# Four graph layers in one kernel: mask and row maximum fused on VectorE, first normalisation on ScalarE, output projection in float32, all orders rewritten, no loop

## The reference

```python
h = jnp.maximum(_layernorm(x, axis=-1), 0.0)
x = x + _L0_gnn_ref(h, L0_gnn_w_qkv, L0_gnn_w_proj, L0_gnn_b_proj, L0_gnn_ln_gamma, L0_gnn_ln_beta, adj)
h = jnp.maximum(_layernorm(x, axis=-1), 0.0)
x = x + _L1_gnn_ref(h, adj, L1_gnn_Wq, L1_gnn_Wk, L1_gnn_Wv)
h = jnp.maximum(_layernorm(x, axis=-1), 0.0)
x = x + _L2_gnn_ref(h, L2_gnn_W, L2_gnn_a, L2_gnn_beta, adj)
h = jnp.maximum(_layernorm(x, axis=-1), 0.0)
x = x + _L3_gnn_ref(h, adj, L3_gnn_weight, L3_gnn_bias)
```

```python
attn = jnp.einsum('bhnd,bhmd->bhnm', q, k) * scale
attn = jnp.where(attn_mask[None, None] == 0, -jnp.inf, attn)
attn = jax.nn.softmax(attn, axis=-1)
o = jnp.einsum('bhnm,bhmd->bhnd', attn, v).transpose(0, 2, 1, 3).reshape(b, n, d)
o = o @ w_proj + b_proj
```

## Time and profile before

| what | value |
|---|---|
| median of 3 runs | 1529.49 us (1529.12 to 1531.04) |
| the profiled execution, its own time | 1527.43 us |
| its span, first to last instruction | 1525.4 us |
| PE busy | 1482.7 us, 97% of the span, 16392 matmuls |
| DVE busy | 1301.0 us, 85% |
| ACT busy | 1120.1 us, 73% |
| POOL busy | 661.3 us, 43% |
| mean granted TensorE clock | 0.994 |

### The profile page before, as it was taken

The page is one execution under the profiler, slowest core; times in us unless marked ns, Lnnn a source line. Parts: engine busy times, 40 slices in busy tenths (PEclk is TensorE's granted clock), DMA queues, the critical chain, the costliest instruction groups (busy, mean ns, idle before and its releaser), DMA issues.

```text
span 1525.4 us, 46270 instructions
## 1 busy us (share of the span) xinstructions
PE 1482.7 (97%) x16392; PEld 1375.0 (90%) x16392; DVE 1301.0 (85%) x3726; ACT 1120.1 (73%) x2884; POOL 661.3 (43%) x981
## 2 busy tenths in 40 slices
PE   6989999999999999999989999999999999999996
PEld 5879999999999999999989999999999999999985
DVE  3888888888888888888888898898898898898895
ACT  4667777777777777777767777777777777777763
POOL 2244444444444444444444444444444444444442
PEclk9999999999999999999999999999999999999999
DMA  3000010000000010000010010010000010000001
GB/s 107 15 16 15 23 30 22 23 29 22 23 30 22 23 29 22 23 29 23 23 31 18 28 29 18 27 30 18 28 30 19 26 30 20 25 29 22 17 16 35
DMA packets 38102, 39.84 MB, mean 26 GB/s; under 512 B 2416, under 2 KB 37488, under 8 KB 37872
## 3 DMA queue, kind: packets, MB, share of 16 engines
q1 hardware_dynamic: 37872, 36.84, 7.9%
HBM read 20.05 MB, written 16.78 MB: 24 GB/s over the span
## 4 chain that ended last, share of the span: by engine, by line
PE 94%; DVE 2%; issue 2%; ACT 1%; POOL 1%; DMA 0%; POOLq 0%; DVEq 0%; ACTq 0%
PE bank L325 41%; PE mid L360 7%; PE mid L325 6%; PE mid L372 5%; PE bank L384 4%; PE mid L388 4%; PE mid L365 4%; PE mid L446 4%; PE mid L534 4%; PE mid L423 4%; PE bank L341 3%; PE bank L474 3%; PE mid L341 2%; PE mid L452 1%; PE bank L458 1%
## 5 line engine op out<-in xcount | busy, mean ns | idle before, releaser
L557 ACT ACTIVATE probs<-mid,neg_max 128x128 f32<-128x128 f32 x1024 | 295.3, 423 | 49.9 <-DVE neg_max L797 49.9
L897 POOL TENSOR_TENSOR rstd<-var_eps,minus_half 128x2 f32<-128x2 f32 x320 | 244.0, 763 | 25.1
L927 POOL TENSOR_TENSOR xb<-x,b_proj_beta 128x512 f32<-128x512 f32 x64 | 82.7, 1293 | 283.1 <-DVE o_res L807 283.1
L895 POOL TENSOR_TENSOR var_eps<-mean_var,eps 128x2 f32<-128x2 f32 x320 | 104.2, 326 | 167.1 <-DVE mean_var L717 167.1
L912 POOL TENSOR_TENSOR inv_norm<-sum_sq,minus_half 128x2 f32<-128x2 f32 x64 | 44.1, 689 | 260.8 <-DVE sum_sq L772 260.8
L730 DVE SCALAR_TENSOR_TENSOR h_t_lo<-bank,h_t_hi 128x512 fp32r<-128x512 f32 x128 | 88.4, 691 | 79.1 <-ACT h_t_hi L650 55.4
L713 DVE BATCH_NORM_STATS2 stats<-x 128x6 f32<-128x256 f32 x384 | 143.3, 414 | 5.8 <-DMA x<-in_x 3.6
L360 PE MATMUL mid<-ident,probs 128*128 128x128 f32 x1024 | 144.0, 275 | 3.7 <-ACT probs L557 3.7
L724 DVE TENSOR_SCALAR z<-x,mean_var,rstd 128x256 f32<-128x256 f32 x384 | 141.2, 410 | 2.7 <-POOL rstd L897 2.7
L360 PEld LDWEIGHTS mid<-ident,probs 128*128 128x128 f32 x1024 | 117.7, 142 | 4.8 <-ACT probs L557 4.8
L384 PE MATMUL bank<-probs_t,v 128*32 128x128 f32 x2048 | 105.9, 278 | 6.6 <-issue 6.0
(11 more groups left out here) (149 smaller groups left out, 5649.5 us busy)
## 6 DMA issues: line engine op xcount, KB each, us to landing
x<-in_x SPq DMA_DIRECT2D x64, 256.0 KB, 2.7
out_x<-x SPq DMA_DIRECT2D x64, 256.0 KB, 2.2
w_qkv_sb<-in_w_qkv SPq DMA_DIRECT2D x1, 768.0 KB, 4.5
w_q_sb<-in_w_q SPq DMA_DIRECT2D x1, 256.0 KB, 4.4
w_k_sb<-in_w_k SPq DMA_DIRECT2D x1, 256.0 KB, 4.7
w_v_sb<-in_w_v_t SPq DMA_DIRECT2D x1, 256.0 KB, 5.6
w_proj_sb<-in_w_proj SPq DMA_DIRECT2D x1, 256.0 KB, 5.8
w_gat_x<-in_w_gat SPq DMA_DIRECT2D x1, 256.0 KB, 6.1
```

The costliest lines, as they stand in the source:

```text
L557: last = act.activation(probs[:, r, s], mid[:, r, s * N:(s + 1) * N], ACT.Exp, bias=neg_max[:, r, s:s + 1])
L895: pool.tensor_tensor(var_eps[:, k], mean_var[:, k, :, 1], eps[:], ALU.add).then_inc(ln_eps[k], 1)
L897: pool.tensor_tensor(rstd[:, k], var_eps[:, k], minus_half[:], ALU.pow).then_inc(ln_rstd[k], 1)
L927: pool.tensor_tensor(xb[:], x0[:, i1], both(b_proj_beta), ALU.add).then_inc(xb_ready, 1)
```

## The change

Five things are changed.

1. **Mask and maximum.** The four mask matmuls are gone and each score matmul writes its own part of the bank (`start=True, stop=True`). `q_t` is scaled by -SCALE, so the banks hold the negated scores. VectorE runs, for each of the 16 heads of a pair, one `tensor_tensor_reduce` that adds +1e30 where there is no edge, stores the sum in `masked` in SBUF, and keeps the minimum of each row as `neg_max`. Ahead of every four of them stands a memset of one element. The program lists each as two instructions: the operation itself, and one that writes out `neg_max`. The two `tensor_reduce` are gone. ScalarE's exponentials read `masked` from SBUF, with scale -1.
2. **First z.** `z0` moves from VectorE to ScalarE, as z = x * rstd + shift with a small `shift0` from VectorE (one instruction of 128 x 2).
3. **Output projection in float32.** `o_t_hi`, `o_t_lo` and the split of `w_proj` are gone; the projection is 4 float32 matmuls of 256 columns in place of 12 in fp32r.
4. **Orders, banks and distances.** Each engine's step is written in a new order, and nearly all products use other banks. The four transposes of probabilities go to banks of their own in place of `mid`. Several parts move to an earlier step of a pair: `q` and `k` to `on[0]`, heads, `rel_v`, `z1` transposes, `hw`, `u` and `y_t` each one step earlier on TensorE. The distance from load to store stays eight steps.
5. **No loop, early constants.** All 71 steps are written out. The late constants are made ahead of step 2 on VectorE and POOL, and TensorE waits for them ahead of step 4 (all three: step 5 before). The fold of `w_q` and `w_k` runs ahead of step 0's transposes on TensorE (ahead of step 1 before).

```diff
-    STEPS = 28
-    FIRST = STREAMS + (PAIRS - STREAMS) % STEPS
...
-            for t in range(FIRST):
+            for t in range(PAIRS + STREAMS - 1):
                 for made_by, make in set_up:
                     if made_by == t:
                         make()
                 step(t, t % 2, streams(t))
-            with eng.Fori(FIRST, PAIRS - STEPS + 1, STEPS) as t:
-                for i in range(STEPS):
-                    step(t + i if i else t, i % 2, [True] * STREAMS)
...
             def scores():
-                for r in range(RG):
-                    pe.matmul(mid[:, r], ident_b[:], mask_b[:].unsqueeze(1).to_broadcast([128, BC, N]),
-                              start=True, stop=False)
...
-                                             k_t[at, hc, b * N:(b + 1) * N], start=False, stop=s == BC - 1,
+                                             k_t[at, hc, b * N:(b + 1) * N], start=True, stop=True,
...
+                if on[2]:
+                    pe.wait_ge(o_norm_ready, done(p2))
+                    bank_free(pe, (o_norm_ready, p2, 1), (probs_t_ready[0], p2, 1))
+                    rows_f32(halves(o_bank), lambda b, c: o_t[:, b, c], w_proj_sb).then_inc(o_psum, 1)
...
-            run(pe, step, [(1, fold), (2, next_weights), (5, last_weights)])
+            run(pe, step, [(0, fold), (2, next_weights), (4, last_weights)])
...
-                    last = act.activation(probs[:, r, s], mid[:, r, s * N:(s + 1) * N], ACT.Exp,
+                    last = act.activation(probs[:, r, s], masked[:, r, s], ACT.Exp, scale=-1.0,
                                           bias=neg_max[:, r, s:s + 1])
...
+                    act.activation(flat(q_t), q_bank, ACT.Copy, scale=-SCALE).then_inc(q_ready, 1)
...
+                    act.wait_ge(shift0_ready, done(p0))
+                    wait_before(act, h_t_psum[0], p0)
+                    for b in range(2):
+                        last = act.activation(z[0][:, b], x0[:, i0, b], ACT.Identity, bias=shift0[:, b:b + 1],
+                                              scale=rstd[:, 0, b:b + 1])
+                    last.then_inc(z_ready[0], 1)
...
+            def least_masked(r):
+
+                dve.memset(mask_turn[:, r:r + 1], 0.0)
+                for s in range(BC):
+                    last = dve.tensor_tensor_reduce(out=masked[:, r, s], in0=mid[:, r, s * N:(s + 1) * N], in1=mask[:],
+                                                    scale=1.0, scalar=LARGE, op0=ALU.add, op1=ALU.min,
+                                                    accum_out=neg_max[:, r, s:s + 1])
+                return last
...
+                if on[0]:
+                    dve.wait_ge(ln_rstd[0], done(p0))
+                    wait_before(dve, z_ready[0], p0)
+                    dve.scalar_tensor_tensor(shift0[:], mean_var[:, 0, :, 0], -1.0, rstd[:, 0], ALU.mult, ALU.mult)\
+                       .then_inc(shift0_ready, 1)
...
-            run(dve, step, [(1, first_constants), (2, next_constants), (5, last_constants)])
+            run(dve, step, [(1, first_constants), (2, next_constants), (2, last_constants)])
...
-            run(pool, step, [(1, next_constants), (5, last_constants)])
+            run(pool, step, [(1, next_constants), (2, last_constants)])
```

More of the change, by code:

```diff
@@ new lines, in step @@
+                if on[4]:
+                    pe.wait_ge(z_ready[2], done(p4))
+                    bank_free(pe, (max_ready[2], p1, 1), (x2_ready, p4, 2), (hw_ready, p5, 2))
+                    transposes(z2_bank, z[2]).then_inc(h_t_psum[2], 1)
+                if on[3]:
+                    pe.wait_ge(g_ready, done(p3))
+                    pe.wait_ge(h1_full_ready, done(p3))
+                    bank_free(pe, (max_ready[3], p1, 1), (probs_t_ready[1], p2, 1))
+                    for b in range(2):
+                        for c in range(C):
+                            last = pe.matmul(rel_bank[:, b * N:(b + 1) * N], h_t1_full[:, c, b * N:(b + 1) * N],
+                                             g_t[:, c, b * N:(b + 1) * N], start=c == 0, stop=c == C - 1)
+                    last.then_inc(rel_psum, 1)
@@ new lines, in step @@
+                if on[5]:
+                    pe.wait_ge(att_norm_ready, done(p5, 2))
+                    bank_free(pe, (max_ready[0], p1, 1), (e_sum_ready, p5, 2), (x3_ready, p6, 1))
+                    for b in range(2):
+                        last = pe.transpose(att_bank[:, b * N:(b + 1) * N], att_norm[:, b], ident[:])
+                    last.then_inc(att_t_psum, 1)
+                if on[1]:
+                    pe.wait_ge(probs_ready[2], done(p1))
+                    bank_free(pe, (g_ready, p3, 1), (y_lo_ready, p7, 1))
+                    transpose_probs(2).then_inc(probs_t_psum[2], 1)
@@ new lines, in step @@
+                if on[3]:
+                    pe.wait_ge(rel_sq_ready, done(p3))
+                    for b in range(2):
+                        last = pe.matmul(rel_bank[:, 256 + b:257 + b], rel_sq[:, b], ones[:, 0:1], start=True, stop=True)
+                    last.then_inc(sum_sq_psum, 1)
+                if on[4]:
+                    pe.wait_ge(h_lo_ready[2], done(p4))
+                    bank_free(pe, (h_lo_ready[2], p4, 1), (max_ready[2], p1, 1), (x2_ready, p4, 2))
+                    bank_free(pe, (max_ready[1], p1, 1), (k_ready, p1, 1))
@@ L448, in step @@
                     last.then_inc(y_t_psum, 1)
+                if on[0]:
+                    pe.wait_ge(h_lo_ready[0], done(p0))
+                    bank_free(pe, (hw_ready, p4, 2), (max_ready[1], p1, 1))
+                    columns(k_bank, w_qkv_p, D, h_t[0]).then_inc(k_psum, 1)
                 if on[4]:
-                    pe.wait_ge(rel_sq_ready, done(p4))
-                    for b in range(2):
-                        last = pe.matmul(rel_bank[:, 256 + b:257 + b], rel_sq[:, b], ones[:, 0:1], start=True, stop=True)
-                    last.then_inc(sum_sq_psum, 1)
-                if on[5]:
-                    pe.wait_ge(hw_ready, done(p5, 2))
-                    bank_free(pe, (hw_ready, p5, 2), (v1_ready, p4, 1), (o_res_ready, p3, 1))
+                    pe.wait_ge(hw_ready, done(p4, 2))
+                    bank_free(pe, (x3_ready, p5, 1), (att_t_ready, p5, 1), (max_ready[0], p1, 1))
                     for b in range(2):
@@ new lines, in step @@
+                if on[7]:
+                    act.wait_ge(shift3_ready, done(p7))
+                    wait_before(act, y_t_psum, p7)
+                    for b in range(2):
+                        last = act.activation(h3[:, b], x3_up[:, i7, b], ACT.Relu, bias=shift3[:, b:b + 1],
+                                              scale=rstd[:, 3, b:b + 1])
+                    last.then_inc(h3_ready, 1)
+                if on[5]:
+                    act.wait_ge(h_t_psum[2], done(p5))
+                    wait_before(act, hw_psum, p5)
+                    act.activation(flat(h_t[2][0]), z2_bank, ACT.Relu).then_inc(h_hi_ready[2], 1)
@@ L613, in step @@
[L613 to L621 removed]
+                    act.wait_ge(hw_psum, done(p5))
```

600 lines of the change are left out of this document (276 added, 324 removed).

## The result

The changed kernel takes 1483.12 us (median of 4 runs, 1480.12 to 1483.83) against 1529.3 us (1527.46 to 1531.04) beside it: a ratio of 0.9697, with a 95% interval of 0.9682 to 0.9712. The profiled execution took 1483.83 us, its span is 1482.0 us, and its mean granted TensorE clock 0.991.

A forecast was written before the change was run, and what follows sets the result against it. TensorE's queue was taken as the bound: 64 steps of 22.34 us (1429.8) plus 51.8 us standing give a span of 1481.6; with time outside the span and the median's offset, 1485 us, range 1466 to 1514.

The forecast's parts named there:

- What bounds: TensorE's queue sets the time: 22.87 us a step before, 22.34 after, with 51.8 us in which it stands.
- Mask: The mask matmuls leave TensorE's step: 0.95 us less, or 0.85 as the bound.
- Projection: On TensorE, 12 two-part matmuls (1.52 us) become four float32 ones (1.74 us), costing 0.22 us a step.
- Entries: Passages on TensorE from float32 to fp32r: 0.10 us each, four where three were, +0.20 us a step.
- rivals 1 and 2: VectorE becomes the bound: fused pitch 0.35 us gives 1547 us (7%); 0.29 to 0.33 gives about 1507 us (8%).
- The five small operations: `shift0` and four one-element memsets added to VectorE's step: 0.5 us together, between nothing and 1 us.
- Hand-overs: Waits between engines fall into place in the new order; narrowest is `k_t`, ready 0.7 us before the scores.
- rival 3: VectorE still stands about 1.7 us a step, so TensorE waits for it: 1517 us, or 1501; 15%.
- First z: `z0` leaves VectorE, 0.64 us less a step there; ScalarE gains two operations of 0.606 us each.
- Loop and constants: The loop edge's 4.55 us and step 5's 6.01 us go; step 2 waits 1.8 us for late constants.
- the sign for step 4: TensorE would stand at step 4 for less than 2 us.
- Drain and fill: Last pair's way 1.2 us shorter, fill within 8 us either way; step 63's end to span's end 5 to 15 shorter.

The follow-up runs named there:

- The control: The kernel before with all steps written out, plus three unused SBUF tiles that shift later tiles' addresses: 1538.40 us against 1524.15 without the tiles.
- e5_k_behind_q: Changed kernel with TensorE's twelve k matmuls directly behind q, ahead of two transpose groups and y_t: 1534.92 us, 1.0042 of the kernel before.

## Why the prediction was right, point by point

The prediction was 1485 us with a range of 1466 to 1514, and the time is 1483.12. The bound, the mask and VectorE's price were read rightly. One term inside the step was too large and was hidden by another that was left out, and the ends came right in sum only. That the step came out within 0.01 us is partly luck.

- **What bounds.** TensorE, before and after. The step was forecast at 22.34 and is 22.33; the time in which it stands at 51.8 and is 52.9.
- **Mask.** Forecast 0.95, measured 0.95 in the new order and 0.86 in the old.
- **Projection.** Float32 forecast at 1.74, measured 1.73. The difference was forecast at 0.22; in the new order it is 0.31, as the two-part form would no longer stand behind the scores.
- **Entries: the step that failed.** The prediction said "so each passage to fp32r costs 0.10", and +0.20 for the step. The price was read at the scores and used everywhere. The chain of the changed kernel gives each block from the end of the one ahead to its own end:

```profile
605.66 0.44 PE bank L348 x4
606.10 1.42 PE bank L313 x12
...
609.16 1.56 PE mid L313 x12
610.72 1.43 PE bank L313 x12
...
613.02 0.89 PE bank L493 x8
613.91 1.42 PE mid L313 x12
```

`q` (610.72) stands behind another two-part block and pays no passage: 1.43. `v1` behind transposes (606.10) and `k` behind `y_t` (613.91) take 1.42, so these two passages are free. `hw` behind `rel_sq` (609.16) takes 1.56, so this one costs 0.1, and so does `v0` behind the scores (first matmul 0.23, next 0.12). In the old order `hw` and the projection paid, and `q` behind `s2` paid a part (0.03 to 0.05). By pitches averaged over 19 steps, the new passages come to about +0.06 over the old ones and not +0.20. What stood in place of the rest is the pitch of blocks that the edit doesn't touch, which the prediction didn't have at all. Without their first matmuls `k` and `v0` take 0.05 to 0.06 longer each than in the kernel before, `v1` 0.03, `g`, `hw` and `q` 0.01 to 0.02, and `y` 0.04 less: together +0.15 a step, 10 us. The control shows that places alone can do this (+0.22 with its tiles); in the changed kernel places and order were not separated. Added up: -0.96 for the mask, +0.21 for the projection, +0.06 and +0.15 make -0.54, and -0.53 was measured.
- **VectorE.** The pitch of the fused operation was forecast at 0.22 and is 0.212; so rivals 1 and 2, which need 0.29 and more, were out. The estimate of 0.258 by the Trainium skill (VectorE: DVE Perf Modes, the section on the TRN2 errata) doesn't agree with this trace, which has a pitch of 0.212 and a listed duration of 0.287. Halving the width of the earlier trace rows did lower the price, by as much as the elements. The five small operations were put at 0.5: `shift0` takes 0.24, and the memsets run inside their neighbours' time. Idle time: forecast 1.1, measured 1.60.
- **Hand-overs.** The waits fell into place; rival 3, with 15%, didn't come. "`k_t` is ready 0.7 us before the scores" holds: its copy ends at 617.98 and the scores start at 618.67. But the prediction missed a place that is as narrow. `q_t` ends at 615.53 behind three other copies on ScalarE, and the transposes of `z1`, which write the bank it is read from, start at 616.26, 0.73 later. With `q_t` 1.4 us later in a step (`e5_k_behind_q`) TensorE lost 0.84 us a step.
- **ScalarE.** At most 19.3 was forecast, 18.5 is measured. The exponentials, for which 1 us more had been allowed, cost 0.7 more. Their listed duration fell from 423 to 391 ns with the source in SBUF, but their pitch rose from 0.249 to 0.293 us, 16 a step: read from a run of them in each kernel, before and now,

```profile
623.12 2.17 ACT L557 ACTIVATE probs<-mid,neg_max 128x128 f32<-128x128 f32 x8 [0.64 <-DVE neg_max L797]
```

```profile
623.43 2.44 ACT L541 ACTIVATE probs<-masked,neg_max 128x128 f32<-128x128 f32 x8
```

(2.17 - 0.42) / 7 = 0.250 and (2.44 - 0.39) / 7 = 0.293. The scale of -1 came in with the source and was not tried apart.
- **First z, orders.** The move of z was counted as 0.64 off VectorE on the way to its sum. It is worth nothing here, since VectorE has more to spare than that; with eight fused operations more on VectorE it was worth 11.6 us. In the old order TensorE didn't wait for the fused mask either. What the new orders bring by themselves was not run alone; the nearest pair, both with a two-part projection and the slower pitch of `k`, is 22.23 us a step (old order) against 22.02 (new).
- **Loop and constants.** 4.55 forecast, 5 measured. TensorE has no idle time of 0.3 us or more between 50 and 145 us, so the sign for step 4 came true. The net 4.2 for the constants (6.0 less 1.8) is 5.0 in the new order; in the old one the clock behind the stop made it 9.7, which the prediction didn't count.
- **Drain and fill.** From the first product of TensorE's step 64 to the end of the span it is 87.8 us before and 81.6 now, 6 shorter, inside the 5 to 15 that were named. But that step opens with `u` before and with the scores now. By the chains, first `u` and the last pair's scores before, then the last pair's scores now:

```profile
1437.61 0.87 PE mid L423 x4
...
1448.44 1.10 PE mid L372 x32
```

```profile
1400.41 1.10 PE mid L357 x32
```

From the last pair's scores to the end it is 77.0 us before and 81.6 now, so the drain behind them is 4.6 longer. What became shorter is the fill: the seventh pair's scores start at 127.3 in place of 140.4, and 8.8 of these 13 us lie between the fourth pair's and the fifth's (18.99 in place of 27.79), where the late constants stood. So the forecast of 51.8 came near by two misses that cancel: the constants gave back more than the 4.2 it counted, and the drain, counted at 1.2 shorter, became longer. TensorE's clock is lower at the end: 0.68 in its last 28 us, where before had 0.87. A late window of the changed kernel:

```profile
1460.00:1480.00 20.00, 12.75 (x58) 11.22 (x58) 7.27 (x19) 5.13 (x12) 4.17 (x5) 0.66 0.08 27
```

The ledger, from runs where one undoes the part and else from the rows: loop -5, constants -5 to -10, mask -60, projection +13 (its 0.21 a step between the two kernels), passages +4, pitch of the untouched blocks +10, first z 0. Together -43 to -48, and -46 was measured. Nothing is left over that would price the new orders by themselves.

## What to carry to other kernels

Move work off the bound engine and price it by a row of the same form at another width, corrected by how like rows fall with width; then ask of every engine not for its busy share but for the queue position of what the bound engine waits for, as one copy that came 1.4 us late cost more than the whole change gained (52 us against 46). When a kernel adds or drops a tile, compare the pitch of untouched matmuls before crediting or blaming the edit: a control run with dead tiles of the same size costs little. A step sum that comes out right is no proof of its terms: undoing them one at a time, and comparing block by block what was not touched, showed which were wrong.

## What the runs showed of the hardware that I had not expected

- Three unused tiles in SBUF (256 bytes, 16 bytes and 8 KB a partition) made the same fp32r matmuls of 256 columns take 0.119 to 0.120 in place of 0.113 us in the blocks of `k` and `v0`, and the kernel took 14 us longer (1538.40 against 1524.15).
- The passage from float32 to fp32r has no fixed cost. Behind `y_t` the first fp32r matmul holds the queue 0.08 us longer and `y_t` 0.08 less (0.81 against 0.89), and behind transposes it is alike; behind the scores and behind `rel_sq` about 0.1 is paid.
- Behind a stop of 6.01 us TensorE was granted the lower clock (0.54 in that window), and the heads took 3.56 us in place of 1.9, so the stop cost 7.7.
- The one-element memsets between VectorE's fused operations took no time of their own: with one listed at 599.92, fused operations start at 599.90 and 600.11, the same 0.21 apart as without it.
- ScalarE's exponentials of 128 x 128 follow each other at 0.249 us when they read PSUM and at 0.293 us when they read SBUF (with a scale of -1 added), although their listed duration is longer from PSUM (423 against 391 ns).
